# Selective scan, layer norms and gated MLP on one core: the jobs of a chunk at other places in the queues, and GpSimd's u*B two units ahead of the scan in place of three

## The reference, cut to what matters

```python
xz = x @ W_xproj.T                        # 64 ranks, 16 B, 16 C
dt = softplus(dt_raw @ W_dt.T + b_dt)     # 256 features
dA = exp(dt[..., None] * A)               # 16 states per feature
dBx = dt[..., None] * B * x[..., None]
h = dA_t * h + dBx_t                      # a scan over the 1024 tokens
y = sum over states of h * C_t            # plus Dp * x
x1 = layernorm(x + y)
gate, up = x1 @ wg.T, x1 @ wu.T           # 768 hidden, int weights / 127
out = layernorm(x1 + (silu(gate) * up) @ wd.T)
```

## Time and profile before

| | us |
|---|---|
| median of three runs | 1814.98 (1813.40 to 1815.38) |
| the profiled execution, its own time | 1815.25 |
| its span, first to last instruction | 1813.5 |
| POOL busy | 1708.6 (94%) |
| PE busy | 1696.5 (94%) |
| DVE busy | 1643.8 (91%) |
| ACT busy | 1634.1 (90%) |
| granted TensorE clock, mean | 0.994 |

### The profile page before, as it was taken

How to read it: one execution, slowest core, us unless ns; L and a number is a source line. 1 busy time by engine, 2 the same in 40 slices (tenths; PEclk the granted TensorE clock), 3 DMA queues, 4 the chain that set the end, 5 groups by cost and what they waited for, 6 DMA issues and landing times.

```text
span 1813.5 us, 31118 instructions
## 1 busy us (share of the span) xinstructions
PE 1696.5 (94%) x11048; PEld 1322.0 (73%) x11048; DVE 1643.8 (91%) x1999; ACT 1634.1 (90%) x3157; POOL 1708.6 (94%) x740
## 2 busy tenths in 40 slices
PE   5789999999999999999999999999999999999987
PEld 3667777777777777777777777777777777777765
DVE  5799999999999999999999999999999999999993
ACT  5799999999999999999999999999999999999983
POOL 4999999999999999999999999999999999999980
PEclk9899999999999999999999999999999999999999
DMA  8232443324443324443324443224443324443210
GB/s 271 89 120 71 153 153 109 101 97 153 153 153 107 98 103 153 153 153 107 105 95 153 153 153 117 81 109 153 153 153 106 98 102 153 153 153 111 78 55 28
DMA packets 116637, 224.77 MB, mean 124 GB/s; under 512 B 11169, under 2 KB 45570, under 8 KB 116482
## 3 DMA queue, kind: packets, MB, share of 16 engines
q1 hardware_dynamic: 116482, 222.78, 36.9%
HBM read 203.87 MB, written 18.87 MB: 123 GB/s over the span
## 4 chain that ended last, share of the span: by engine, by line
ACT 48%; PE 30%; DVE 15%; issue 6%; DMA 0%; DVEq 0%; ACTq 0%; SPq 0%
ACT ub_t L562 12%; ACT p_da L544 10%; DVE h L761 10%; ACT da_k L544 10%; PE p_m L1042 9%; PE p_o L1067 5%; PE p_da L976 5%; PE p_y L1009 4%; ACT x L575 3%; ACT L588 2%; DVE x_t L790 2%; ACT dt L522 2%; ACT x_t L580 2%; PE p_m L942 2%; DVE hid L795 1%
## 5 line engine op out<-in xcount | busy, mean ns | idle before, releaser
L445 POOL TENSOR_TENSOR h<-h,c_bc 128x1024 f32<-128x1024 f32 x416 | 982.3, 2380 | 25.5 <-ACT h_carry L531 19.5
L434 POOL TENSOR_TENSOR ub<-u,b_bc 128x1024 f32<-128x1024 f32 x287 | 682.2, 2384 | 33.7 <-DVE u L811 22.0
L1009 PE MATMUL p_y<-ident,h 128*128 128x128 f32 x4096 | 521.0, 274 | 6.1 <-POOL h L445 3.8
L1009 PEld LDWEIGHTS p_y<-ident,h 128*128 128x128 f32 x4096 | 468.4, 142 | 56.6 <-POOL h L445 13.5
L544 ACT ACTIVATE p_da<-dt,neg_a 128x512 f32<-128x512 f32 x576 | 393.5, 683 | 64.4 <-DVE h L761 62.7
L562 ACT ACTIVATE ub_t<-u_t,bc_t 128x256 f32<-128x256 f32 x896 | 397.8, 496 | 2.3 <-PE p_da L976 2.3
L761 DVE TENSOR_TENSOR_SCAN h<-p_da,ub 128x512 f32<-128x512 f32 x288 | 340.3, 1208 | 22.1 <-ACT p_da L544 20.6
L761 DVE TENSOR_TENSOR_SCAN h<-p_da,h_carry,ub 128x512 f32<-128x512 f32 x288 | 353.6, 1265 | 4.6 <-ACT p_da L544 4.0
L1067 PE MATMUL p_o<-wt_down,hid 128*128 128x256 f32 x1488 | 344.4, 381 | 0.0
L976 PE MATMUL p_da<-ident,ub_t 128*128 128x128 f32 x1792 | 267.8, 279 | 55.8 <-DVE h L761 54.6
L544 ACT ACTIVATE da_k<-dt,neg_a 128x512 f32<-128x512 f32 x448 | 319.0, 713 | 0.4
(11 more groups left out here) (98 smaller groups left out, 1591.5 us busy)
## 6 DMA issues: line engine op xcount, KB each, us to landing
c_bc<-bc_rows_dram SPq DMA_DIRECT2D x416, 256.0 KB, 6.8
b_bc<-bc_rows_dram SPq DMA_DIRECT2D x96, 512.0 KB, 6.4
b_bc<-bc_rows_dram SPq DMA_DIRECT2D x32, 768.0 KB, 3.9
x_in<-in_L_attn_x SPq DMA_DIRECT2D x32, 512.0 KB, 8.5
out_x<-res_n SPq DMA_DIRECT2D x31, 512.0 KB, 3.3
bc_rows_dram<-bc_rows SPq DMA_DIRECT2D x32, 64.0 KB, 6.1
hid<-in_L_ffn_w_gate SPq DMA_DIRECT2D x1, 768.0 KB, 4.9
hid<-in_L_ffn_w_up SPq DMA_DIRECT2D x1, 768.0 KB, 6.7
```

What stands on the lines that cost most here:

```text
L434: nc.gpsimd.tensor_tensor(ub[:, ub_slot(c, i), :, :], u[:, par, :, :], b_bc[:, i:i + 1, :].broadcast_to([P, DH, T]), ALU.mult).then_inc(s_ ...
L445: nc.gpsimd.tensor_tensor(h[:, s % H_SLOTS, :, :], h[:, s % H_SLOTS, :, :], c_bc[:, i:i + 1, :].broadcast_to([P, DH, T]), ALU.mult).then_i ...
L1009: ins = nc.tensor.matmul(p_y_tok[:, k, q * P:(q + 1) * P], h[:, s % H_SLOTS, q, k * P:(k + 1) * P], ident[:, :], start=(s == SUM_ORDER[0] ...
```

## The change

Only constants change. Two things move on GpSimd: every `ub` one unit later, and the job `u_of` from (8, 1) to (10, 0). Some forty places in `AT` change by one or a few zones; many of them name the same position in a queue as before. The SP queue holds the store behind the broadcasts of units 5 to 9, where it stood ahead of them, and ACT makes the `da_k` of state 3 one unit earlier.

```diff
-UB_AHEAD = 3
+UB_AHEAD = 2
...
 AT = {
-    "weights": (7, 1), "x_transposed": (0, 3), "x_out": (0, 3), "project": (2, 2), "rank_out": (3, 1),
...
+    "weights": (7, 1), "x_transposed": (0, 3), "x_out": (0, 0), "project": (1, 4), "rank_out": (2, 2),
...
 K_STATES = (3, 6, 7, 10, 13, 14, 15)
 K_AHEAD = 2
 K_SLOTS = 2
-LATE = 10
-STORE_AT = 5
-DA_LEAD = {6: 3, 7: 3, 10: 3, 13: 2, 14: 2}
+LATE = 12
+STORE_AT = 10
+DA_LEAD = {3: 2, 6: 3, 7: 3, 10: 3, 13: 2, 14: 2}
 UB_SLOTS = 3
 H_SLOTS = 8
```

More of the change, by code:

```diff
@@ L34 @@
 AT = {
-    "weights": (7, 1), "x_transposed": (0, 3), "x_out": (0, 3), "project": (2, 2), "rank_out": (3, 1),
[L36 to L39, removed]
[9 rows of a table removed]
+    "weights": (7, 1), "x_transposed": (0, 3), "x_out": (0, 0), "project": (1, 4), "rank_out": (2, 2),
+    "bc_out": (2, 0), "project_dt": (4, 0), "softplus_abs": (5, 1), "softplus_exp": (5, 2),
+    "softplus_log": (5, 3), "dt_of": (7, 2), "u_of": (10, 0), "u_transposed0": (12, 0), "u_out0": (13, 3),
+    "u_transposed1": (14, 3), "u_out1": (14, 1), "z_out": (2, 2), "stats1": (3, 2), "mean1": (4, 2),
+    "norm_log": (5, 1), "norm_exp": (5, 2), "shifts": (6, 1), "norm1_0": (5, 3), "norm1_1": (6, 0),
[9 rows of a table added]
 }
```

## The result

The changed kernel takes 1804.61 us, median of four runs (1804.00 to 1805.97). The kernel before took 1815.18 beside it (four runs, 1813.40 to 1816.47). The ratio is 0.9943 with a 95% interval of 0.9926 to 0.9961: faster by some 10 us, against 8.6 forecast (1806.5). The profiled execution took 1805.97, its span is 1804.2, and the mean granted TensorE clock was 0.997, so the clock (0.994 before) is no part of the story.

A forecast was written before the change was run, and what follows sets the result against it. A ring of ACT, PE and DVE, not GpSimd, was taken to set the pace. Even chunks 10.0, odd -1.6, start -0.35, end 0.5: together 8.6 us gained from 1815.25, a median of 1806.5; range 1802 to 1811.

The forecast's parts named there:

- x_out earlier: ACT's copy of x moved ahead of the decay of state 1: 0.38 us gained per even chunk, nothing in odd ones.
- second silu ahead of norm2_0: On ACT, second silu 0.5 us sooner, so the fourth gate waits less: 0.19 us gained per even chunk, none in odd.
- bc_cols between the silus: ACT's column copy moved to where ACT waits for gates, off the way to scan 12's decay: 0.1 us gained per chunk.
- softplus and first norm: Softplus and norm jobs reordered on ACT: the same jobs, costed at nothing.
- SP's order: SP's store behind seven more broadcasts: these land sooner, the load behind has a chunk of time; costed at nothing.
- all other places: Projections, downs, ups, da_k of state 3 and similar moves, mostly in dense PE stretches: costed at nothing.
- GpSimd's order: GpSimd meets state 13's carry, so state 6's product comes 1.2 us later, delaying odd-chunk gates: 0.2 us lost each.
- the slower rival: State 6's product holds the sum before odd-chunk gates, 1.2 us each if uncovered: 1822; chance 0.23, late ubs included.
- Both signs: Signs of being wrong: POOL (GpSimd) in the chain, and gates beginning on PE a microsecond behind the low part.
- GpSimd's floor: Rival: the ring shortens until GpSimd is dense, pair 107.0, 30.1 us gained, 1785 or anything up to 1802; chance 0.13.
- Start and end: First chunk: 1.2 us lost by x_out, about 0.85 gained by turning u earlier; last chunk: 0.5 gained by norm1_3.
- the case that comes to "about nothing": Low case: 0.38 and two small gains at half, GpSimd loss at 0.4: gain 5.0 - 4.8 - 0.35 + 0.5.

The follow-up runs named there:

- before with the two orders: Kernel before with only the change's softplus, norm, silu, norm2_0 and bc_cols places, GpSimd's queue as before: 1800.83 us, ratio 0.9925.

## Why the prediction came out right

The number was right, but not for its reasons alone. This is the ledger of a pair, in us, plus for longer. "Undone" is what putting the places back in the changed kernel cost, with its sign turned.

| step | predicted | measured |
|---|---|---|
| x_out earlier | -0.38 | 0.00 undone |
| second silu ahead of norm2_0 | -0.19 | -0.26 undone (0.54 - 0.28) |
| bc_cols between the silus | -0.20 | -0.28 undone |
| softplus and first norm | 0 | -0.35 undone |
| SP's order | 0 | -0.03 undone, not to be told from nothing |
| all other places | 0 | -0.12 (1.16 - 1.04, with GpSimd's old order) |
| GpSimd's order | +0.20 | +0.24 alone, +0.56 in the changed kernel |
| sum | -0.57 | -0.60 for the whole change |

The measured rows don't add up to -0.60, since each was measured beside other places. With GpSimd's order left as before they do: 1.04 for the two orders on ACT and 0.12 for all the rest are gained, and GpSimd's new order takes 0.56 back.

How far the even chunk has come, counted from the start of its scan 0 (us, medians of nine pairs):

| kernel | decay of state 4 | decay of state 5 | high part of x1 | first hidden |
|---|---|---|---|---|
| before | 10.47 | 13.82 | 27.75 | 37.53 |
| changed | 10.16 | 13.70 | 27.35 | 36.93 |
| changed, x_out back | 10.33 | 13.71 | 27.36 | 36.94 |
| changed, softplus and norm back | 10.17 | 13.70 | 27.65 | 37.23 |
| before with the two orders | 10.46 | 13.82 | 27.45 | 37.04 |

The first hidden comes 0.60 us earlier, which is all of the pair's gain: the odd chunk adds nothing in the changed kernel.

**x_out: the step failed.** It said that of 0.5 us at most 0.38 comes through at ACT's decay of state 4, since that decay needs scan 3 and "ACT has no other idle time there". Scan 0 and scan 4 on DVE and the decays of states 4 and 5 on ACT, in the changed kernel:

```profile
893.62 2.31 DVE L761 TENSOR_TENSOR_SCAN h<-p_da,ub 128x512 f32<-128x512 f32 x2
...
903.79 0.69 ACT L544 ACTIVATE p_da<-dt,neg_a 128x512 f32<-128x512 f32 x1
...
906.08 2.32 DVE L761 TENSOR_TENSOR_SCAN h<-p_da,ub 128x512 f32<-128x512 f32 x2
...
907.32 0.69 ACT L544 ACTIVATE p_da<-dt,neg_a 128x512 f32<-128x512 f32 x1
```

The same four with x_out back:

```profile
893.00 2.32 DVE L761 TENSOR_TENSOR_SCAN h<-p_da,ub 128x512 f32<-128x512 f32 x2
...
903.33 0.69 ACT L544 ACTIVATE p_da<-dt,neg_a 128x512 f32<-128x512 f32 x1
...
905.46 2.32 DVE L761 TENSOR_TENSOR_SCAN h<-p_da,ub 128x512 f32<-128x512 f32 x2
...
906.71 0.69 ACT L544 ACTIVATE p_da<-dt,neg_a 128x512 f32<-128x512 f32 x1
```

With x_out early the decay of state 4 starts 10.17 us behind scan 0, with x_out back 10.33: 0.16 is gained there. The decay of state 5 needs the first half of scan 4, and that scan starts 12.46 us behind scan 0 in both; half of its 2.32 us later, the decay follows at 13.70 and 13.71. So the gain ends one handover behind the place where the prediction stopped counting: ACT comes earlier and stands for DVE. The high part did come 0.40 us earlier, close to the 0.38 forecast, but not by x_out, as the table shows: 0.30 of it goes with the softplus and norm order, and 0.1 with the other places at the start of the chunk (13.82 to 13.70, with x_out early or late). DVE's wait for the high part tells the same: 1.14 us before, 0.94 in the changed kernel, 0.85 with x_out back, and 1.13 with the softplus and norm order back; 0.76 had been predicted. x_out alone on the kernel before was not tried.

**Softplus and norm: a term of the sum left out.** "The same jobs" was true and not enough. The order decides how often an instruction stands right behind its source. 0.35 per pair is nearly what x_out failed to give, so the two errors cancelled: that the sum of the pair came out is luck to this extent.

**silu and bc_cols: the mechanism right, the sizes small.** The gates went from 3.83 to 3.63 as said, and back to 3.83 where the silus were put back. Both terms gave some 40% more than predicted; `bc_cols` delivers the whole 0.16 us of its queue time per chunk in the even chunk, and 0.28 in the pair.

**GpSimd: place, mechanism and size right for the kernel before, too small for the changed one.** The carry of state 13, the product of state 6 and the sum ahead of the gates are where they were predicted. Alone, the loss is 0.24. But the slower rival was nearer than its chance: with the low part ready sooner, the sum holds the gates, 0.56 us per pair. This rival said that 1.2 us is the price if nothing covers it; half of that was paid. Both signs that it would leave, GpSimd in the chain and gates 0.88 us behind the low part (869.45 - 868.57), are in the profile, while the time came out as forecast: a sign can be seen and the sum still hold, where other terms pay for it. The changed kernel lost some 8 us in this way.

**GpSimd's floor.** It wasn't reached in any run. The fastest pair is 107.70 against 107.0. The Trainium skill ("Perfetto Trace Analysis", Identifying the Most-Contended Engine) says to work first on the engine with the highest occupancy. The trace does not bear it out for the kernel before: with the queues of GpSimd, PE and DVE untouched, two orders on ACT brought the time to 0.9925 of it. It fits the changed one, where GpSimd leads the chain and its old order alone gave 8.0 us. The share of busy time was 94 and 95% and could not tell these two apart; the chain did.

**Start and end.** From dt of chunk 0 to that of chunk 1 the kernel lost 1.30 us (29.44 to 30.74), near the 1.2 predicted for x_out. But putting x_out back returns 0.70 of it (30.04), or 0.49 with `UB_AHEAD` at 3, and putting the softplus and norm order back returns 1.07 (29.67): again the size is right and only about half of it is x_out's. The next chunk gained 2.5 us, where 0.85 was predicted for the turning of u ahead of the weights; which of the places does it was not tested, only that the two orders alone don't (107.92 - 50.99 = 56.9 there, 56.1 before, 53.6 in the changed kernel). The end lost 0.4, where a gain of 0.5 was predicted. Start and end together: 0.8 gained, 0.15 predicted.

**A slip in the sum.** In the case that comes to "about nothing" the odd chunks stand with -4.8, which counts `bc_cols` whole; at half, as the text says, it is 16 x (0.05 - 0.4) = -5.6, and the case is 0.45 us slower in place of 0.35 faster. Neither the forecast nor a bound rests on it.

## What to carry to other kernels

Price a moved job at the places where another engine hands over, not in its own queue, and follow it through the next one too: an earlier start that passes one decay and is taken back at the decay behind it is worth nothing, and 0.16 us between two decays that a scan waits for is worth all of it. When several engines are at 90% and more, look which one the chain names, and after each gain look again: an edit that costs 0.24 us alone cost 0.56 once the others had their gain, so the parts of a bundle must be undone one by one on the bundle, not only tried one by one on the kernel before. In a dense queue of ACT, don't let an instruction stand right behind the one it reads from.

## What the runs showed of the hardware

- ACT starts an instruction that reads the result of the one right ahead of it 0.13 us later than another: 1.08 against 0.95 us for 128x1024 float32, 0.34 against 0.21 behind a 128x8 one. Over all chunks of the kernel before and the changed one it was 1.07 to 1.10 against 0.94 to 0.96, and 0.32 to 0.36 against 0.19 to 0.21, one at 0.31. The profile shows it as neither idle time nor as a wait.
- That alone was not undone apart from the rest of the softplus and norm order. The order gave ACT 0.29 us a chunk; of a pair 0.35 were seen under GpSimd's new order, 0.30 of it in the even chunk, while the odd chunk gives its part back at the sum of state 6.
- GpSimd's product of 128x1024 float32 took 2.32 to 2.33 us from one to the next in both orders of its queue, next to `ub` or to its like.
